# A local-attention and global-attention block: all images' global attention as one stream of units, the next image's earlier stages in small steps beside it

## What is computed

```python
x = x + L0(_gn(x))          # _gn: group norm, 32 groups of 4 channels
t = tokens(x)               # per image: 3136 tokens of 128 numbers
t = t + L1(_ln_t(t))        # _ln_t: layer norm over the 128 numbers
t = t + (_ln_t(t) @ w_lora.T) @ W.T

# L0: 16 heads of 8; each token attends to its 7x7 window, with a bias per head and offset
l = einsum('bhijd,bhijd->bhij', q, kac) + bias      # for each of the 49 offsets
attn = softmax(logits, axis=-1)                     # over the 49

# L1: 8 heads of 16; each token attends to all 3136 tokens of its image
scores = einsum('bhqd,bhkd->bhqk', q, k) * scale
weights = softmax(scores, axis=-1)
attn = einsum('bhqk,bhkd->bhqd', weights, v)
```

## Time and profile before

| | us |
|---|---|
| three timed runs | 10115.39, 10139.77, 10154.37 (median 10139.77) |
| the profiled execution | 10123.25 |
| its span, on which all rows count | 10121.2 |
| first scores of an attention stretch | 434.3 |

### The profile page before, as it was taken

One profiled execution on the slowest core, in us unless ns is written; L12 is line 12 of the kernel. 1 busy time (PEld: TensorE's weight loads), 2 busy tenths in 40 slices (PEclk: granted clock), 3 DMA queues, 4 the chain that ended last, 5 costly groups with the idle time before them and its releaser, 6 DMA issues.

```text
span 10121.2 us, 420263 instructions
## 1 busy us (share of the span) xinstructions
PE 8905.5 (88%) x166082; PEld 4676.6 (46%) x166082; DVE 7995.4 (79%) x13637; ACT 6473.8 (64%) x13361; POOL 1653.8 (16%) x1701
## 2 busy tenths in 40 slices
PE   6799977999779996799977999679997799977999
PEld 5344453444534445344453444534445344463444
DVE  6799767997679966799667996679966799667996
ACT  3388834888348883488834888348883488834887
POOL 5100051000510005100051000510005100060000
PEclk9799987999879998799987999879998799987999
DMA  4300043000430004300043000430004300042000
GB/s 74 59 3 3 3 70 57 3 3 3 71 56 3 3 3 71 55 3 3 3 73 53 3 3 3 74 52 3 3 3 74 52 3 3 3 77 50 3 3 9
DMA packets 386621, 276.39 MB, mean 27 GB/s; under 512 B 49836, under 2 KB 377244, under 8 KB 383516
## 3 DMA queue, kind: packets, MB, share of 16 engines
q1 hardware_dynamic: 378524, 229.58, 13.9%
q0 software_dynamic: 6144, 19.28, 1.2%
HBM read 144.03 MB, written 25.86 MB: 17 GB/s over the span
## 4 chain that ended last, share of the span: by engine, by line
PE 78%; issue 11%; DVE 3%; SPq 3%; ACT 2%; DMA 1%; POOL 1%; ACTq 0%; DVEq 0%; POOLq 0%
PE PS L666 21%; PE PS L729 20%; PE PS L707 20%; PE PS L590 4%; PE PS L601 4%; PE PS L612 3%; SPq L400 2%; DVE block_max L1094 2%; ACT arena L898 1%; PE PS L635 1%; PE PS L697 1%; PE PS L693 1%; PE PS L639 1%; PE PS L561 1%; PE PS L630 1%
## 5 line engine op out<-in xcount | busy, mean ns | idle before, releaser
L1062 DVE TENSOR_REDUCE block_max<-PS 128x1 f32<-128x448 f32 x10192 | 5691.1, 618 | 489.0 <-PE PS L666 361.8
L898 ACT ACTIVATE arena<-PS 128x448 f32<-128x448 f32 (+1 forms) x11200 | 5259.7, 559 | 1158.5 <-PE PS L729 1133.4
L666 PE MATMUL PS<-KP,arena 96*32 96x448 bf16 x43904 | 4107.3, 372 | 359.0 <-DMA KP<-arena 282.1
L729 PE MATMUL PS<-arena,KP 99*32 99x448 bf16 x43904 | 3997.1, 354 | 110.5 <-ACT arena L898 75.7
L707 PE MATMUL PS<-arena 128*32 128x448 f32 x22400 | 2631.3, 539 | 19.3 <-ACT arena L898 14.9
L666 PEld LDWEIGHTS PS<-KP,arena 96*32 96x32 bf16 x43904 | 1233.3, 98 | 2084.9 <-issue 544.9
L729 PEld LDWEIGHTS PS<-arena,KP 99*32 99x32 bf16 x43904 | 1227.4, 96 | 1684.4 <-ACT arena L898 905.6
L827 ACT ACTIVATE arena<-PS 80x512 f32<-80x512 f32 (+1 forms) x896 | 428.8, 538 | 1036.7 <-PE PS L601 1035.7
L513 POOL CAST shift_parts<-shift 14x128 bf16<-14x128 f32 x112 | 31.5, 281 | 5427.7 <-ACT shift L864 5427.7
L707 PEld LDWEIGHTS PS<-arena 128*32 128x32 f32 x22400 | 681.4, 110 | 385.7 <-ACT arena L898 90.6
L986 DVE TENSOR_TENSOR arena<-PS,nat_bias 128x80 f32<-128x80 f32 (+3 forms) x1120 | 354.1, 383 | 498.6 <-PE PS L590 498.4
(11 more groups left out here) (97 smaller groups left out, 4382.3 us busy)
## 6 DMA issues: line engine op xcount, KB each, us to landing
arena<-vT_padded SPq DMA_DIRECT2D x1792, 70.0 KB
arena<-arena SPq DMA_DIRECT2D x384, 98.0 KB, 4.3
KP<-arena POOLq DMA_DIRECT2D x192, 98.0 KB, 8.1
KP<-arena SPq DMA_DIRECT2D x192, 98.0 KB, 4.4
arena<-in_x SPq DMA_DIRECT2D x9, 1568.0 KB, 6.5
vT_padded<-arena SPq DMA_DIRECT2D x16, 784.0 KB
out_y<-X SPq DMA_DIRECT2D x56, 224.0 KB, 2.4
arena<-shift_parts SPq DMA_DIRECT2D x336, 3.5 KB
```

The lines of the kernel that those rows point to most:

```text
L666: ins = mm(PS[at:at + QT, bank, 0:BLK], QP[0:ROWS, g, unit_queries(unit, h, t, QT)], KP[0:ROWS, g, h, j * BLK:(j + 1) * BLK], start=True, ...
L729: ins = mm(PS[k0:k0 + 32, at % banks, 0:BLK], KP[0:ROWSM, g, h, c * P + k0:c * P + k0 + 32], QP[0:ROWSM, g, unit_queries(unit, h)], start= ...
L898: nc.scalar.activation(exp_buffer(c)[0:n, h, :], PS[0:n, bank, 0:BLK], ACT.Exp, scale=float(ADIM) ** -0.5).then_inc(exp_done, 1)
L1062: V.tensor_reduce(block_max[:, q, j:j + 1], PS[:, max_banks()[0][m][0], 0:BLK], AX.X, ALU.max).then_inc(max_read, 1)
```

## The change

The order of work is now made by a small planner, `Plan`. Time in it is counted in chunks of the attention stream: an image has 14 x 25 = 350, each with two places (sub 0 after the second score group, sub 1 after the fourth) where a side task may stand. Side tasks share one PSUM bank (7). PE waits before each side task until the bank's last reader is done (`side_read`).

- The front of the first image runs alone (`Plan(True, None)`, bank number n % 8). Then the attention units of all images follow each other (`each_image`: kinds "first", "middle" in a `Fori` over six images, "last", "after"). Beside image b's units stand all front stages of image b + 1, b's own unit tails, and the last layer norm and feed-forward of b, of which the last block stands beside the next image's first unit.
- A strip takes nine chunks (`PERIOD`): three pieces of scores, row maxima, subtraction, exponentials, sum, inverse and product, and for the strip before four pieces of transposes and one of values. `VP`, `PT` and `QB` have one buffer, `SC` two.
- Maxima for unit k + 1 (from chunk 21 on, k + 2) are made across image seams as well, in three banks. The separate first-maxima stretch is there once.
- The normalised x is made per block of 448, twice (for keys and values, and again for queries). The other dense matmuls are cut into four column tiles of 32 (`across`).
- POOL makes the split into three bf16 parts, per block. Parts go to DRAM (`q_dram`, `k_dram`) and come from there into `QP` (four slots of one unit each) and `KP`; the values of the global attention go by `v_dram` into `VA`. `X2` holds the next image's x; a DMA copies it to `X`.
- The `arena` is gone: each tile has its own region. The value stacks have 17 columns a head instead of 32.

```diff
-            with pe.Fori(0, images) as b:
...
+class Plan:
+    def tails(self, attention):
+        units = {"first": range(1, AUNITS), "after": range(1)}.get(attention, range(AUNITS))
+        for k in units:
+            t = k * CHUNKS
+            self.fix(t + 1, 1, "spread", k)
+            self.fix(t + 2, 0, "invert", k)
+            self.fix(t + 2, 1, "normalise_unit", k)
+            self.fix(t + 3, 1, "project", k)
+            if k == 0 or k > NBLK:
+                i = (k - 1 - NBLK) % NBLK
+                self.fix(t + 5, 1, "mean3", i)
...
+                self.fix(t + 10, 1, "ffn", i)
+                self.fix(t + 12, 0, "store_out", i)
...
+    def place(self, t, task, i):
+        sub = 0
+        while (t, sub) in self.taken:
+            t, sub = t + sub, 1 - sub
+        self.fix(t, sub, task, i)
+        return t
+
+    def front(self):
...
+        for s in range(STRIPS):
+            t = FIRST_STRIP + PERIOD * s
+            for n in range(3):
+                self.fix(t + n, 0, "scores", 3 * s + n)
+            self.fix(t + 3, 0, "maxima", s)
+            self.fix(t + 4, 0, "subtract", s)
+            self.fix(t + 5, 1, "exponentials", s)
+            self.fix(t + 6, 0, "sum_up", s)
+            self.fix(t + 8, 0, "invert_strip", s)
+            self.fix(t + 8, 1, "normalise", s)
+            for c in range(4):
+                self.fix(t + PERIOD + 3 + c, 0, "turn", 4 * s + c)
+            self.fix(t + 2 * PERIOD - 1, 0, "values", s)
+            self.fix(t - 4, 0, "spread_queries", s)
+            self.fix(t + (PERIOD if s else 0), 0, "load_windows", s)
...
+                def store_parts(dram, parts, split, stored, j):
+                    wait(sp, stored, of(b, ahead, 16 * NBLK, 16 * j))
+                    wait(sp, split, of(b, ahead, 4 * NBLK, 4 * j + 4))
+                    sp.dma_start(image_of(dram, b, ahead).rearrange("b m c t -> c (b m) t")[:, :, j * BLK:(j + 1) * BLK],
+                                 parts[:, :, :]).then_inc(stored, 16)
...
+                def load_k(g):
+                    of_image = ahead if g == 0 else 0
+                    wait(sp, k_out, of(b, of_image, 16 * NBLK, 16 * NBLK))
+                    if ahead == 1:
+                        wait(sp, st_ready, of(b, 0, AUNITS * GH * CHUNKS, (1 - g) * NBLK * GH * CHUNKS))
+                    for n, m in enumerate(K_PARTS):
+                        src = image_of(k_dram, b, of_image)[:, m, g * GH * ADIM:(g + 1) * GH * ADIM, :] \
+                            .rearrange("b (h e) t -> e (b h) t", e=ADIM)
+                        sp.dma_start(KP[n * ADIM:(n + 1) * ADIM, g, :, :], src).then_inc(keys_in[g], 16)
...
+            def across(bank, weights, rhs, n=BLK):
+                for at in range(0, P, 32):
+                    ins = mm(PS[at:at + 32, bank, 0:n], weights[:, at:at + 32], rhs, start=True, stop=True,
+                             tile_position=(0, at))
+                return ins
...
+                def beside(t, sub):
+                    if (t, sub) in plan.taken:
+                        pe.wait_ge(*side_read(b, 1, *previous[0]))
+                        apart(pe)
+                        do(*plan.taken[t, sub], SIDE_BANK)
+                        previous[0] = plan.taken[t, sub]
...
+                for k in range(AUNITS):
+                    for c in range(CHUNKS):
...
+                        maxima(1)
+                        if c == 0:
+                            pe.wait_ge(shift_in, of(b, 0, AUNITS * 48, (k + 1) * 48))
+                        for h in range(GH):
+                            scores_turned(k, c, h)
+                            if h == 1:
+                                beside(k * CHUNKS + c, 0)
+                            if h == 2 and c > 0:
+                                weigh(k, c - 1)
+                            if h == 2 and c == 0 and (k > 0 or kind != "first"):
+                                weigh(k - 1, CHUNKS - 1)
+                            if h == 3:
+                                beside(k * CHUNKS + c, 1)
+                            maxima(1)
+                        maxima(len(steps))
```

More of the change, by code:

```diff
@@ L177, in hybrid_block @@
[L177 to L186, removed]
-        VTs = part(6608, 28 * P).rearrange("p (c e) -> p c e", c=28)
@@ L270, in apart, with wait, of @@
+        def wait(eng, s, value):
+            if not isinstance(value, int) or value > 0:
+                eng.wait_ge(s, value)
+            if eng is nc.sync and not isinstance(value, int):
+                apart(eng)
         def apart(eng):
             eng.sem_inc(paced, 1)
+        def of(b, ahead, per, at):
+            return b * per + (ahead * per + at)
         def blk(t, j):
             return t[:, j * BLK:(j + 1) * BLK]
-        def unit_index(b, unit):
-            g, i = unit
-            return b * AUNITS + (g * NBLK + i)
@@ new lines, in hybrid_block, with alone_bank, each_image @@
+        alone = Plan(True, None)
+        plans = {name: Plan(name in ("first", "middle"), name) for name in ("first", "middle", "last", "after")}
+        ALONE_SLOTS = max(t for t, sub in alone.at) + 1
+        def alone_bank(task, i):
+            return alone.order.index((task, i)) % 8
+        def each_image(eng, image):
+            image(0, "first")
+            if images > 2:
+                with eng.Fori(1, images - 1) as b:
+                    image(b, "middle")
+            image(images - 1, "last")
+            image(images, "after")
@@ new lines, in side, with image @@
+                return do
+            do = side(0, 0)
+            for t in range(ALONE_SLOTS):
+                for sub in range(2):
+                    for task, i in alone.at[t, sub]:
+                        do(task, i)
+            do("split_max", 0)
+            def image(b, kind):
+                do = side(b, 1)
+                for t in range(AUNITS * CHUNKS):
+                    for sub in range(2):
+                        for task, i in plans[kind].at[t, sub]:
+                            do(task, i)
@@ L542, in _ @@
+            each_image(pool, image)
         @block.tensor
@@ L910, in _ @@
+                            if c == 0 and h == 1 and (k > 0 or kind != "first"):
+                                read_sums(k - 1)
+                            if h == 1:
+                                beside(k * CHUNKS + c, 0)
+                            if h == 3:
+                                beside(k * CHUNKS + c, 1)
+            each_image(act, image)
         @block.vector
```

1563 lines of the change are left out of this document (918 added, 645 removed).

## The result

The changed kernel takes 10,020.8 us (median of four runs, 10013.14 to 10028.66) against 10,137.9 us of the kernel before, measured beside it (10115.39 to 10154.37). The ratio is 0.9886 with a 95% interval of 0.9865 to 0.9907: 1.1% faster, where 8% was forecast (9310) and 9940 was the upper end of the range. The profiled execution has a span of 10022.9 us.

What follows compares the result with a forecast made beforehand. PE was taken to bound the attention stretch, handing work round the rest. Start 490 + 7 periods of 1135 + last image 850 + tail 14 = 9299 us span, about 9310 shown; own range 9085 to 9610, with rivals 8850 to 9940.

Steps and rivals of the forecast that it cites:

- PE's sum: PE's own work for one image in the stream, all at full clock, switching included: 1066 us.
- the middle that I took for the score pieces: Cost of switching to 32x32 tiles for 84 score pieces, between bounds 0 and 0.30 us each: 13 us an image.
- The idle allowance: PE idle per image: 24 us kept from today's stretch, 30 for DVE's unevenness, 15 for shift and late code.
- more waits could cost 0.1 each: Upper bound for the 156 inserted column-tile pieces: 16 us an image, counted as nothing in the sum.
- DVE's unevenness: DVE-heavy strip chunks hold up PE through three banks of maxima: 30 us an image, bounds 0 and 50.
- The late shift: Shift chain queued on POOL and SP delays PE at a unit's first score: 15 us an image together with late code.
- the rival of handing over in order: A late shift stops PE, then DVE and ACT: 70 us an image, period 1205, total 9789; chance 0.15.
- PE starves for code: Late code costs 9.5 ns per matmul, 158 us an image: period about 1280, total 10,310, slower than before; chance 0.08.
- The head: First image's front runs alone; stream starts at 490 us, bounds 430 and 600, against 434 today.
- Tables and round trips: In the first front, waiting for bias tables and DRAM round trips, against 35 us of copying saved: +24 us.
- The strips: In the first front, one strip's cycle takes up to 9.8 us against 8.65: +32 us.
- The last image and the tail: After seven periods, the last image takes 850 us and one remaining tail block with its store 14 us.

Runs made afterwards that it cites:

- c5: Changed kernel with windows, keys, values and x loads cut to a fraction of their bytes, output not the reference's: 9,735.7 us, one run.
- c1: Changed kernel with a strip's 112 value matmuls, and DVE's mask, cut into two pieces in neighbouring chunks: 9,879.0 us, one run.
- a3: Changed kernel with ACT's readers of the side bank (negate_max, invert) moved into the place where PE writes: 9,852.9 us, one run.
- a2: Changed kernel with DVE's strip row maximum and sum halved and the sum over heads moved one place later: 10,000.5 us, one run.
- f2: e1 with the first image's query loads issued right behind the first keys, before the values: 9,506.5 us, ratio to before 0.937.
- e1: Changed kernel plus a3, c1, spread loads, reordered first front, halved DVE row maxima and sums, and halved strip exponentials on ACT: 9,539.7 us.

## Why the prediction was wrong

The main mechanism was right: 435 us of stages in series went beside attention, and each engine's work came out close to its sum. Two terms were wrong, PE's idle time in the period and the head, and they took six sevenths of the gain. The forecast span was 9299; measured were 606.6 + 8547 (seven periods) + 847 + 22 = 10,023. Of the 724 us between them, 117 lie ahead of the stream, 602 in the seven periods, 5 at the end.

1. **PE's sum (1066).** Right in kind, 26 too high. Changing to the whole array costs 0.20, not 0.30 (22 an image, not 34); the middle that I took for the score pieces (13) was near the 0.18 measured (84 x 0.18 = 15). Groups and `weigh` have the cadence of the earlier trace rows.
2. **The idle allowance (24 + 30 + 15 = 69).** This is the step that failed. Measured idle is 189. 51.5 of it are gaps, nearly all of them waits for code, where the 15 were to hold late code and the shift together. Transfers make about half (c5: -25), the value burst nearly half (c1: -22; how far the two overlap was not run). Another 23.6 are the side bank (a3), a wait that is in the diff (`side_read`) and that I named only as "more waits could cost 0.1 each", at the pieces with column tiles. I asked what stands behind a waiting PE, but not where its releaser stands in ACT's own queue. Of the 120 us too much, the gaps are 36.5 and the side bank 23.6; the other 60 are small waits and pauses between groups, and no run shows what they would give back.
3. **DVE's unevenness (30).** PE does wait for DVE's banks, 90.7 us in the image of the rows below, part of it beside other work. But the lumps of the strips don't set the period: halving them gave 1.6 (a2), for ACT's bank took over. What the term is worth stays open.
4. **The late shift** (part of the 15, and the rival of handing over in order). Nearly free. Ahead of L1005's matmuls and weight loads the shift's transfers stand with 9.1 us in the whole run, and 8.8 of these are the head's own, at 606.57. The rival's total of 9789 was nearer than mine, for another reason.
5. **PE starves for code** (0.08). The phenomenon is there, as the code packets show, and the price was too high: 51.5 us an image, not 158. It had come from 9.5 ns per short matmul; 51.5 / 16,700 is 3 ns. I gave the burst and the DMA one price, and put it on the DMA; the runs show two causes. Taken at its measured size in the sum it would have moved the forecast by 7 x 37 = 260 us, within 450 of the result.
6. **The head (490).** Tables and round trips were +24 and are +22: the first scores of a strip come at 91.2 instead of 69.1, and the hole of 60.4 takes the place of 35.4 and of the dense middle stages. The strips were +32 and are +150: 27 of them take 356.5 us, against 206.0 in the first image before (13.2 each against 7.6). I had set the strip alone to 9.8, from the 8.65 of the earlier trace rows, as if engines handed on at once. One cycle of a strip:

```profile
293.87 1.32 DVE L1323 TENSOR_REDUCE SUMS<-SC 128x14 f32<-128x1120 f32 x1 [3.34 <-ACT SC L1098]
294.21 1.40 PE L834 MATMUL PS<-PT,VP 96*32 96x32 f32 x101 [2.58 <-ACT PT L1104]
298.14 0.43 PE L834 MATMUL PS<-PT,VP 96*32 96x32 f32 x11 [2.53 <-issue]
298.50 3.51 PE L815 MATMUL PS<-Kn,QB 32*32 32x80 f32 x112
298.60 0.62 DVE L1333 TENSOR_TENSOR PVM<-PS,C 128x448 f32<-128x448 f32 x1 [3.41 <-PE PS L834]
299.26 0.99 DVE L1344 TENSOR_REDUCE On<-PVM 128x112 f32<-128x448 f32 x1
300.17 0.23 DVE L1328 RECIPROCAL SUMS<-SUMS 128x14 f32<-128x14 f32 x1
300.48 2.06 POOL L687 TENSOR_TENSOR SC<-SC,SUMS 128x1120 f32<-128x1120 f32 x1 [6.77 <-DVE SUMS L1328]
302.64 1.80 PE L824 MATMUL PS<-C,SC 128*80 128x128 f32 x14 [0.63 <-issue]
```

The reader is to see DVE's order at work. The sum is done at 295.2, but the reciprocal stands behind the value product of the strip before, so it waits for PE's values and for a gap of 2.5 us inside them; POOL and PE's turns wait for the reciprocal. PE's scores take 3.51 us for 112, against 1.94 for 102 in the earlier trace rows: from 298.5 to 302.0 the granted clock was 0.59, much of it the lower of its two levels (1.2 GHz). In the stream the same order holds up nothing: none of the waits ahead of L824 there is for POOL.

7. **The last image and the tail** (850 and 14): 847 and 22.

What stays open: in f2 the period is still 1160.7 - 1040 = 121 above PE's own steps, 19 of them gaps. The waits of one image of the changed kernel name PE's three banks on each side (engine, line, waited for: us, times, longest):

```profile
PEld PS L943 <- DVE block_max L1448: 90.7, 291, 1.3
...
PEld PS L1005 <- ACT PB L1221: 45.6, 139, 1.1
```

They are many small waits, of which some overlap work. Half lumps on DVE (a2) moved them from one bank to the other, and half lumps on ACT (e1) gave nothing back. Whether more banks would was not tried.

The Trainium skill (Runtime: NRT & Kernel Launch, Instruction fetch mechanics) says that code fetch is hidden because an engine issues more slowly than the fetch fills. The trace agrees for the attention stretch of the kernel before, where the same count finds 1.1 us of gaps in 832 us. It differs beside large loads and behind 112 matmuls and as many weight loads in 0.98 us, with 51.5 us an image; the measurement decides.

## What to carry to other kernels

Laying a front stage beside a full engine is worth what that engine's idle time shrinks, so forecast the idle time as carefully as the sum: for each shared buffer, write down where its reader stands in the reader's own queue, and put the reader into the writer's place. Look at the code's own queue in the trace where an engine pauses and no semaphore stands; here it paid to cut a run of very short matmuls into pieces (22.8 us a period) and large loads into parts (12.3). Issue first what is needed first: a queue that is held by a large transfer holds all behind it.

## What the hardware showed

- Code can be late, and the trace shows it: 90% of the time of the gaps ends 1 to 2 us after a 16 KiB packet of the queue `q8 instruction`. It happens with little DMA traffic too: 26 us of gaps an image remained with most bytes of the loads gone (c5), and they fell from 51.5 to 29.2 when one burst of 112 short matmuls was cut in two (c1). The gap comes often after the burst, in other instructions.
- One matmul of a group can stand 7.48 us behind its neighbour (at 4152.90). The code packet before it started 16.7 us after the last one, where 6.5 is the median, with the DMA 96% busy. These long gaps, 15.4 us an image in sum, were all gone in c5.
- Issuing a transfer held SyncE while the DMA was full (0.96 busy): 20.57 us for one small transfer behind 816 KB, 24.23 us for twelve of 56 KB behind six of 392 KB.
- Changing between column tiles and the whole array cost 0.20 us there and back with four-matmul groups around it, to 32x32 tiles 0.18, between column-tile shapes nothing.
